# Four graph layers on one core: the SAGE products in fp16 pairs scaled on chip, and GAT's edge counts moved into its logits

## What is computed

```python
# layer 1: two SAGE layers (deg_inv = 1 / max(number of edges into a node, 1))
def _sage_layer(h, edge_src, edge_dst, deg_inv, W_self, W_neigh, b):
    agg = segment_sum(h[edge_src], edge_dst)
    return h @ W_self + (agg * deg_inv[:, None]) @ W_neigh + b
h = relu(_sage_layer(x, ..., W_self0, W_neigh0, b0))
out = _sage_layer(h, ..., W_self1, W_neigh1, b1)
# layer 2: GAT, 4 heads of 64, after rms norm and W_down
act = leaky_relu(xl[src] + xr[dst], 0.2)
e = einsum('ehd,hd->eh', act, att)
p = exp(e - segment_max(e, dst)[dst])
alpha = p / (segment_sum(p, dst)[dst] + 1e-16)
out = segment_sum(alpha * xl[src], dst) @ W_up
```

## Time and profile before

| | us |
|---|---|
| median of 3 runs | 3811.01 (3806.96 to 3817.25) |
| the profiled execution | 3811.61 |
| its span, first to last instruction | 3809.9 |
| PE busy in the span | 3487.1 |
| DVE, POOL, ACT busy | 1925.3, 1237.3, 904.2 |
| mean granted clock of PE | 0.956 |

### The profile page before, as it was taken

One profiled execution on the slowest core, in us unless ns is written; L12 is line 12 of the kernel. 1 busy time (PEld: TensorE's weight loads), 2 busy tenths in 40 slices (PEclk: granted clock), 3 DMA queues, 4 the chain that ended last, 5 costly groups with the idle time before them and its releaser, 6 DMA issues.

```text
span 3809.9 us, 55179 instructions
## 1 busy us (share of the span) xinstructions
PE 3487.1 (92%) x22747; PEld 2907.5 (76%) x22747; DVE 1925.3 (51%) x4210; ACT 904.2 (24%) x1340; POOL 1237.3 (32%) x947
## 2 busy tenths in 40 slices
PE   5899079999999799999999699999999999999988
PEld 4665058999999799987778596777777777777788
DVE  7864155221333354455545497676764444444467
ACT  0111024111201211221111394332312222222224
POOL 2677633322333027776677562200000000000021
PEclk8999589999999899999999899999999999999999
DMA  8588862556422435455544557442341222221233
GB/s 291 140 263 244 244 201 65 131 126 142 121 59 51 167 102 161 153 169 185 164 145 144 185 218 269 173 139 81 123 141 56 90 76 81 77 87 67 68 100 104
DMA packets 270889, 533.95 MB, mean 140 GB/s; under 512 B 86587, under 2 KB 135730, under 8 KB 268618
## 3 DMA queue, kind: packets, MB, share of 16 engines
q1 hardware_dynamic: 145526, 400.68, 31.0%
q0 software_dynamic: 74080, 52.74, 8.7%
q10 hardware_dynamic: 51030, 77.00, 5.8%
HBM read 352.66 MB, written 177.63 MB: 139 GB/s over the span
## 4 chain that ended last, share of the span: by engine, by line
PE 60%; DMA 12%; POOL 10%; DVE 7%; issue 6%; ACT 4%; SPq 0%; POOLq 0%; ACTq 0%; DVEq 0%
PE ps L393 40%; PE ps L721 14%; DMA EM<-ee,adr 6%; POOL gr L2151 3%; POOL EM L2141 3%; POOL gl L2151 3%; PE ps L483 3%; DMA T<-cnt,adr 2%; ACT pb L1908 2%; DVE eqj L882 1%; POOL T L2114 1%; DVE eqj L879 1%; DMA slab<-T 1%; PE ps L398 1%; ACT pt L1922 1%
## 5 line engine op out<-in xcount | busy, mean ns | idle before, releaser
L721 PE MATMUL ps<-mh,whl 128*128 128x384 f16 (+5 forms) x2560 | 528.5, 300 | 20.3 <-DVE gs L1391 14.4
L393 PE MATMUL ps<-wb,xth 128*128 128x256 f32 (+1 forms) x2560 | 460.8, 282 | 7.1 <-DVE xtl L1056 5.2
L2114 POOL DMA_INDIRECT TR<-cnt,adr x167 | 270.8, 1621 | 541.2 <-DMA TR<-cnt,adr 509.6
L393 PEld LDWEIGHTS ps<-wb,xth 128*128 128x128 f32 (+1 forms) x2560 | 389.2, 186 | 8.1 <-DVE xtl L1056 5.4
L2189 POOL TENSOR_TENSOR graw<-graw,rsb 128x1280 f32<-128x1280 f32 (+1 forms) x2 | 5.6, 2822 | 1166.8 <-DMA graw<-GD 1166.8
L721 PE MATMUL ps<-ml,whl 128*128 128x384 f16 (+5 forms) x1280 | 383.0, 299 | 0.0
L721 PEld LDWEIGHTS ps<-mh,whl 128*128 128x128 f16 (+1 forms) x2560 | 289.1, 117 | 92.7 <-issue 14.5
L393 PE MATMUL ps<-wb,xtl 128*128 128x256 f32 (+1 forms) x1280 | 358.5, 280 | 0.0
L393 PE MATMUL ps<-a,yy 128*128 128x384 f16 (+4 forms) x2560 | 343.7, 297 | 6.5 <-DVE yy L1403 5.2
L393 PE MATMUL ps<-a,xhb 128*128 128x384 f16 (+5 forms) x1280 | 341.0, 296 | 0.0
L393 PE MATMUL ps<-a,xob 128*128 128x384 f16 (+5 forms) x1280 | 339.8, 296 | 0.0
(11 more groups left out here) (308 smaller groups left out, 6974.1 us busy)
## 6 DMA issues: line engine op xcount, KB each, us to landing
TR<-zero_w SPq DMA_DIRECT2D x80, 625.0 KB, 3.8
wraw<-in_L_gnn_weight SPq DMA_DIRECT2D x64, 512.0 KB, 3.3
EM<-neg SPq DMA_DIRECT2D x10, 2500.0 KB, 21.8
ar<-TR SPq DMA_DIRECT2D x72, 320.0 KB
eb<-EM SPq DMA_DIRECT2D x9, 2500.0 KB, 9.1
ar<-TR SPq DMA_DIRECT2D x72, 305.0 KB
UD<-ue ACTq DMA_DIRECT2D x72, 256.0 KB, 3.2
uu<-UD SPq DMA_DIRECT2D x36, 512.0 KB, 6.9
```

What stands on the lines that cost most here:

```text
L393: i = pe.matmul(ap, l, r, start=(q == 0), stop=(q == len(pairs) - 1))
L721: ins = pe.matmul(ps[:, 0:cn], l, r, start=(q == 0), stop=(q == len(pairs) - 1))
L2114: return pool.indirect_dma_start(out=flat, out_offset=bass.IndirectOffsetOnAxis(ap=adr[:, n, t:t + 1], axis=0), in_=cnt[:, n, t:t + 1], in ...
```

## The change

Its parts:

1. The operands of all SAGE matmuls (am, hhi, hlo, wb, and x as xh16, xl16) are fp16. As fp16 has a small range, x1 is scaled by XS = 1024, the weights by YS = 56 over their largest magnitude, and the hidden layer by a bound made of the largest weights and the largest bias. The largest magnitudes are found on chip: SP loads every weight of a layer once more in 16 pieces of 512 KB (ww_), DVE reduces each (layer 0's in the loop over the tiles of x1, layer 1's in layer 0's finish steps), PE turns and spreads the result, and `scales` makes the scale vectors. The results are unscaled in the finish steps (und, dn).
2. Copies and subtractions of these operands turn into multiplications by a scale (ACT) and scalar_tensor_tensor (DVE).
3. In SP's order, weights of the next quarter are loaded earlier (W_neigh at the start of a quarter, W_self after its fifth tile).
4. The counts of GAT: instead of multiplying exp(e - max) by the count, log(count) is added to the logit. POOL gathers the count of each edge from BD (`times`, 167 indirect transfers between the adds to TR, from add 20 on one each, and two each in the last 20); SP reads BD's diagonal (`load_loops`, ten transfers of single elements, ahead of the first SAGE weights); DVE waits for the counts after tile 5 of x2T, ACT takes the logarithms after tile 7; DVE adds them to each batch of logits. The root for the rms norm moves from the end of x2T to its beginning.
5. In the softmax stage nb and the multiplications are gone, eb has three buffers, and the maxima of tiles 1 to 9 are taken over all heads at once by halving (m1, m2, m3), one or two tiles ahead. DVE copies the second group of pt too for heads 0 to 2. For head 3 POOL copies the logits into pb first and exp works in place. The rows of x2 for the next stage are loaded in another order.

```diff
-        am = at("am", [128, NT, N], F32R, O + 78.5)
+        am = at("am", [128, NT, N], F16, O + 78.5)
-        hhi = at("hhi", [128, NT, 256], F32R, O + 127.5)
+        hhi = at("hhi", [128, NT, 256], F16, O + 127.5)
...
+            def largest_piece(layer, j):
+                w.wait_ge(*ww_in[layer][j % 2](j))
+                dve.tensor_reduce(out=wm[:, layer, j:j + 1], in_=ww_[layer][j % 2][:, :, :], axis=AX.XY, op=ALU.max,
+                                  apply_absolute_value=True).then_inc(*V.tick("wm", layer, j))
...
-                    dve.tensor_tensor(wb[n][:, 1, :, c], wp[a][:, :, :], wb[n][:, 0, :, c].bitcast(F32),
-                                      ALU.subtract).then_inc(*V.tick("wp", w_turn[0] - 1))
+                    dve.scalar_tensor_tensor(out=wb[n][:, 1, :, c], in0=wp[a][:, :, :], scalar=ssc[:, layer, n:n + 1],
+                                             in1=wb[n][:, 0, :, c], op0=ALU.mult, op1=ALU.subtract).then_inc(
+                        *V.tick("wp", w_turn[0] - 1))
...
             for i in range(NT):
                 turned_rows("x2T", i)
+                if i == 5:
+                    rsqrt(dve, w, rms[:, :], vpe[:, :], t10[:, :], "rms")
+                    w.wait_ge(*cg_in("cg"))
+                    dve.tensor_scalar(out=cg[:, :], in0=cg[:, :], scalar1=1.0, scalar2=None, op0=ALU.max).then_inc(*V.tick("cg"))
...
+                w.wait_ge(*A("cg"))
+                dve.tensor_tensor(ee[:, t0:t0 + m, :], ee[:, t0:t0 + m, :], cg[:, t0:t0 + m, None].broadcast_to([EP, m, 4]),
+                                  ALU.add).then_inc(*V.tick("ee", b))
...
+                if part == 0:
+                    w.wait_ge(*em_in[a](i))
+                    dve.tensor_tensor(m1[0:r, :, :], eb[a][0:r, 0:625, :], eb[a][0:r, 625:1250, :], ALU.max).then_inc(*V.tick())
+                elif part == 1:
+                    dve.tensor_tensor(m2[0:r, :, :], m1[0:r, 0:313, :], m1[0:r, 312:625, :], ALU.max).then_inc(*V.tick())
+                else:
+                    dve.tensor_tensor(m3[0:r, :, :], m2[0:r, 0:157, :], m2[0:r, 156:313, :], ALU.max).then_inc(*V.tick())
...
+                if i == 7:
+
+                    w.wait_ge(*dg_in("dg"))
+                    for r, c in ((128, slice(0, 9)), (98, slice(9, 10))):
+                        act.activation(dg[0:r, c], dg[0:r, c], ACT.Ln).then_inc(*A.tick("dg"))
+                    w.wait_ge(*V("cg"))
+                    act.activation(cg[:, :], cg[:, :], ACT.Ln).then_inc(*A.tick("cg"))
...
+            def times(t):
+
+                w.wait_ge(*bd_out("bd"))
+                pool.indirect_dma_start(
+                    out=cg[:, t:t + 1], out_offset=None, in_=BD.rearrange("a b -> (a b)").rearrange("(c d) -> c d", d=1),
+                    in_offset=bass.IndirectOffsetOnAxis(ap=adr[:, 0, t:t + 1], axis=0)).then_inc(*cg_in.tick("cg"))
+
             for t in range(ET):
                 w.wait_ge(*tr_add.now())
                 w.wait_ge(*V("adr", 1, min(t // 34 * 34 + 33, ET - 1)))
                 add_counts(TR, 1, t, RPAD * N - 1).then_inc(*tr_add.tick("last"))
+                for c in range(*((t - 20, t - 19) if t < 147 else (2 * t - 167, 2 * t - 165))):
+                    if c >= 0:
+                        times(c)
...
-                    pool.tensor_tensor(pb[n][0:r, :], pb[n][0:r, :], nb[a][0:r, :], ALU.mult).then_inc(*G.tick("weighed", i, h))
...
+            def load_loops():
+                w.wait_ge(*V("rsqrt", "dis"))
+                for i in range(NT):
+                    a0, r = 128 * i * (N + 1), ROWS[i]
+                    sp.dma_start(dg[0:r, i:i + 1], BD.rearrange("a b -> (a b)").rearrange("(c d) -> c d", d=1)[
+                        a0:a0 + (r - 1) * (N + 1) + 1:N + 1, :], allow_slow_non_contiguous=True).then_inc(*dg_in.tick("dg"))
```

More of the change, by code:

```diff
@@ L48 @@
 NS, NU = 11, 4
+HS = 1024 * YS
 NMX = 16 * (NREL - NBR)
@@ L209, in program @@
         up_in, up_out = landed("up_in"), landed("up_out")
+        ww_in = [[landed(f"ww_in{layer}{i}") for i in range(2)] for layer in range(2)]
         wd_in, xl_out, ed_out = landed("wd_in"), landed("xl_out"), landed("ed_out")
@@ L491, in tensor, with largest_weights, spread_weights @@
             turn_rows("xT", 9, zt[9 % NX])
+            def largest_weights(layer):
+                ps = psum.take("wl", layer)
+                w.wait_ge(*V("wl", layer))
+                w.wait_ge(*psum.empty("wl", layer))
+                pe.transpose(ps[0:2, 0:128], wl_[:, layer, 0:2], ident[:, :]).then_inc(*P.tick("wl", layer))
+            def spread_weights(layer):
+                ps = psum.take("ws", layer)
+                w.wait_ge(*V("wlm", layer))
+                w.wait_ge(*psum.empty("ws", layer))
+                pe.matmul(ps[:, 0:2], wl_[0:2, layer, 2:3].broadcast_to([2, 128]), ident[0:2, 0:2], start=True, stop=True).then_inc(
+                    *P.tick("ws", layer))
             for d in TURN_D:
                 r = ROWS[d]
+                if d == TURN_D[1]:
+                    largest_weights(0)
+                if d == TURN_D[3]:
+                    spread_weights(0)
                 for g in range(3):
@@ L1125, in vector @@
                     V.at["hlo", layer, q] = V.n
+                    if layer == 0 and q == 2:
+                        largest_over_rows(1)
+                    if layer == 0 and q == 3:
+                        scales(1)
                     for i in range(NT):
@@ L1300, in vector @@
                 dve.tensor_copy(pt[n][0:98, 1:2, 0:r], four(ps, r)[0:98, 1:2]).then_inc(*t)
-                if h == 1:
-                    weigh_late(i)
-                if i + 1 < NT:
-                    maxima(i + 1, h)
+                for j, part in EARLY_MX.get(g, ()):
+                    maxima(j, part)
+                if i > 1 and h > 0:
+                    maxima(i + 2, h - 1)
                 if h == 2 and i > 0:
@@ L1757, in scalar @@
                         w.wait_ge(*P("hn", layer, q, i))
-                        copy(hhi[0:r, i, :], psum.at("hn", layer, q, i)[0:r, 0:256], "hhi", layer, q, i)
+                        act.mul(hhi[0:r, i, :], psum.at("hn", layer, q, i)[0:r, 0:256], 1.0 / (HS if layer else XS)).then_inc(
+                            *A.tick("hhi", layer, q, i))
                         if q == 0 and i == 8:
@@ L1914, in scalar @@
                 r = ROWS[i]
-                for k0 in range(2):
+                for k0 in range(1 if h < 3 else 2):
                     n = (3 * g + k0) % NPT
```

274 lines of the change are left out of this document (197 added, 77 removed).

## The result

The changed kernel takes 3788.0 us (median of 5 runs, 3787.39 to 3801.05), the kernel before beside it 3807.83: a ratio of 0.9956, 95% interval [0.9938, 0.9974]. So the change brings 5 to 20 us by the medians, at most about three fifths of the 32.7 forecast; 3788 lies inside the range of 3753 to 3823. The profiled execution took 3787.45 us, span 3785.7.

What follows compares the result with a forecast made beforehand. PE's matmul issue interval was taken to bound the SAGE layers, PE and GpSimd's chain nearly equally the logits. Terms -50.7 + 3 + 18 + 2 - 5 = -32.7 took 3811.6 to 3779 us, range 3753 to 3823.

Steps and rivals of the forecast that it cites:

- Step 1: SAGE matmuls in fp16: 5440 matmuls at 109.0 in place of 118.4 ns, -50.7 us, bounds 0 and -51.
- step 2: Producers of the fp16 operands on ScalarE and VectorE: covered by idle time, so nothing except at layer 0's start.
- Step 3: Search for the largest weights in both SAGE layers: extra loads and VectorE reduces cost PE nothing.
- Step 4: Start of SAGE layer 0: small VectorE instructions and ten diagonal gathers delay it, +3 us, bounds 0 and +8.
- Step 5: GpSimd's TR chain delayed by loads and gathers: counts complete at 1313 us, 15 late in x2T; +18 us, bounds 0 and +67.
- Step 6: Logarithms of the counts on ScalarE in x2T, a table load and three short instructions: +2 us, bounds 0 and +4.
- Step 7: Softmax: PE bound at 3.43 us per head, so only its start gains, -5 us, bounds 0 and -20.
- (c): Rival: softmax bound by ScalarE, -20 us in place of -5, 3764 us; chance 0.05.
- (a): Rival: loads cost the TR chain under 1 us each, counts land by 1298 in time, 3761 us; chance 0.22.
- (b): Rival: gathers queue behind adds to TR, counts land at 1360, 62 us late, 3826 us; chance 0.13.
- (d): Rival: fp16 matmul interval unchanged in the SAGE layers, nothing late, 3812 us; chance 0.05.

Runs made afterwards that it cites:

- e5: The changed kernel itself, run again in a second set beside the kernel before: 3804.91 us, ratio 0.9991.
- e6: The kernel before, unchanged, traced on the same chip as the second set of runs: median 3809.65 us.
- e10: The changed kernel without the 167 gathers of counts, counts taken as 1, weight loads kept: ratio to before 0.9933.
- e9: The kernel before with the softmax's weighing by counts (waits, loads, multiplications) left out: 3886.07 us, ratio 0.9993.
- e7: The changed kernel with VectorE's wait for the counts moved to just ahead of the logits, ScalarE's logarithm later too: 3774.61 us, ratio 0.9901.
- e8: The changed kernel with the counts' wait moved, softmax maxima reordered and GpSimd's fourth-head copies waiting for their tile's maxima: 3764.98 us, ratio 0.9873.
- e1: The changed kernel with the wait for the counts moved to just ahead of the logits, on a slower chip: 3883.4 us, ratio 0.9968.
- e4: The changed kernel without the 32 weight loads and their reduces, largest weight taken as 0.2: 3881.06 us, ratio 0.9959.
- e12: The changed kernel with the counts' wait moved and GpSimd's fourth-head copies waiting for their tile's maxima, order of maxima kept: ratio 0.9916.

## Why the forecast was right in sign and its gain too large

**Step 1 held** in its size per matmul: 109.2 ns against the forecast's 109.0. From the first SAGE matmul to the last sum it is 619.7 us in place of 666.1: -46.4 in the first pair of profiles, and -46.3 in e5 against e6 (619.4 and 665.7). Of the 4 us missing from 50.7, two are idle time of PE before these matmuls, for VectorE's low halves of x and of the weights: 9.2 us in the page's group, against 7.1 before. So "nothing" in **step 2** was 2 us too little; the other two have no row of their own. **Step 3** held: between 531 and 616 us VectorE is busy 50.8 us and PE 81.2 (82.1 before, over the same times). **Step 4** was +3 and is +0.4: from the end of the z matmuls to the first SAGE matmul 25.2 against 24.8 us. The ten loads of the diagonal took SP 4.6 us, as reckoned, and no one waited for them:

```profile
615.63 4.61 SPq L2487 DMA_DIRECT2D dg<-BD  x10
620.28 2.26 SPq L2500 DMA_DIRECT2D wp<-in_L_gnn_W_neigh  x2
```

The rule of the Trainium skill (DMA: Bandwidth & Descriptors, Rules for kernel authors), one descriptor per element, would by the forecast's estimate have put the term near +8. How long these loads took to land no row shows; they have until x2T, and the weight loads behind them on SP were not late.

**Step 5 is the step that failed, in its size.** Its mechanism is what happened. The term that was too small is the delay of the chain. It was taken as 59 us; from first to last add the chain took 882.9 us in place of 810.2 in the first pair of profiles, 73 more, and 893.5 in place of 826.9 in e5 and e6, 67 more. cg was forecast complete at 1313 us in the old trace's time and was at 1318.7 in an execution that was 6 us early: 12 us late. That is as much as the two adds lost that ran into the loads behind the SAGE layers (11.5 us), for which the forecast has no term beyond its 3 us for busy cycles; the loads' part, 45, is 52 in e10 against e9, which also runs into those loads. The forecast also rests on one trace, and that trace has the shortest chain of all that have neither loads nor gathers, by 17 us.

The other side, when the counts are needed, was about right. The forecast took it from the place where PE begins xd's second chunk, 1298. PE had gone on until 1295.2, which is 1301 in the old trace's time. So PE stood for 25.0 us where 15 were forecast, and the price was 27.5 where 18 stood; in e5, 37.5 and 38.9.

VectorE's own wait is longer than PE's, 31 us in place of the 15 that the forecast named as its sign, because VectorE runs ahead of PE. In the old trace it went on from tile 5 to the next tiles at once:

```profile
1334.30 3.67 DVE L1003 TENSOR_TENSOR xtl<-ps,xth 128x512 fp32r<-128x512 f32 x6
```

so the place of the wait was passed at 1337, not 1346, and with the 47 us of steps 1 and 4 taken off that is 1290; it asked at 1287.8. When VectorE began to wait PE still had work for 7.4 us, which count in the wait and not in its price. Between the two executions the wait and its price moved with the chain's end, which came 11 us later in e5. By the traces, one of each, that is most of why the same change was worth 20 us in one set of runs and 5 in the next.

**Step 6** held: with the wait away (e7, e8), the stage is 93.5 us against 91.1 and 91.6, some +2 us; a table load of 1.28 us and the short logarithms lie in it. **Step 7** was -5 and is -0.6: in the first pair of profiles PE's first turn came 5.4 us earlier after the eb load, exactly as forecast, and was given back by z3 (146.8 us from that turn, 142.0 before), to what the forecast's own lower bound named, the late maxima of tile 1, and those of tile 2 besides. Most of these 5 us show as slower work: over the stretch PE is idle 5.7 us in place of 5.3, but busy 141.1 in place of 136.8, at a granted clock of 0.74 over the first 40 us. My figure of 3.43 us per head was also too long: it added two busy times that overlap. In the changed kernel the weight loads start 3.28 us apart from head to head:

```profile
2217.31 1.12 PEld L422 LDWEIGHTS ps<-ident,pb 128*128 128x128 f32 x10
2218.41 2.31 PEld L417 LDWEIGHTS ps<-xlx,pt 128*128 128x128 f32 x20
2220.59 1.12 PEld L422 LDWEIGHTS ps<-ident,pb 128*128 128x128 f32 x10
```

so 40 heads are at most 131 us. In the kernel before the heads are as far apart (turns at 2187.23, 2190.51 and 2193.79 us), and the other 11 of its 142 us are 5.3 us of idle time, spread over start, tiles and end, the turns of gn (the normalised sums, once per tile), and the lower clock of the first 11 us (0.56). "Heads below 3.3 us would prove (c)" was therefore no test: they were that already. PE is the bound in the middle; the start was not, and e8 takes 7 us out of it.

**The sum** in terms measured from the first pair: -46.4 + 0.4 + 27.5 + 2.4 - 1.4 (the logits' stage, 759.5 us against 760.9 from first gather to last put) - 0.6 (last put to z3) = -18.1, against -19.8 by the medians. For e5 against e6: -46.3 - 0.1 + 38.9 + 1.9 + 7.7 (763.6 us against 755.9) - 1.9 (162.2 against 164.1) = +0.2, where the medians say -4.7. What makes the logits' stage 8 to 12 us longer than e6's in e5, e7 and e8 and 1 us shorter in the first profile stays open; one small VectorE instruction per batch was added to it, and the stage of the kernel before itself took 760.9 and 755.9 us.

**Rivals.** (a), cg in time, did not hold, but e7, whose edit makes it hold, took 3774.6 us, 35 us below before, where (a) reckoned with 51: steps 1 and 7 gave less, and the stage of logits was 11 us longer. (b), gathers behind adds, did not: gathers alone cost the chain 14 us. The rule of the Trainium skill beside it (DMA: Bandwidth & Descriptors, SWDGE vs HWDGE vs iDMA), rings served in turn, is in keeping with the loads' effect on the adds, 1.6 us for 512 KB, which is far from what (b) needed; no run shows the turns themselves. (c) fell by the changed kernel and e8, as said under e9, and (d) by the interval of 109 ns.

## What to carry to other kernels

When an edit adds a wait, read two times from the old trace. The length of the wait counts from when the waiting engine gets there, which its own timeline shows; an in-order engine that runs ahead will stand for the whole difference. The price counts from when the next engine would have needed what stands behind the wait: here 31 us of wait, 25 us of idle PE, 27.5 us of stage. Put a late value's wait as close to its first use as the program allows: here one moved wait was worth 30 us, more than half of what the fp16 operands brought. And a serial chain that ran hidden beside a stage becomes the bound when the stage gets shorter and the chain longer by the same edit; take both off the slack before the sum is made, and ask what the chain will run into once it ends later. How much a hidden chain varies does not show in the time: here it is 17 us between executions of the same code, so read it in more than one trace.

## What the runs showed of the hardware

- VectorE's maximum of two fp32 tensors (128x2500 elements) takes 2.76 us alone (e8), 4.44 us (e7) and 4.78 us (the changed kernel) when it starts during a GpSimd copy of 128x1250, and one of 128x628 takes 0.81 us alone and 2.50 beside such a copy. In both rows of e7 the copy runs on for 1.8 us, and VectorE's instruction takes 1.7 us longer: it loses nearly all of the time in which the two overlap.
- On the two chips with 3903 us, PE, ScalarE and VectorE have waits in the stage of logits that nothing in the profile ends, under "issue". The waits of e1 in its stretch of logits:

```profile
ACT ue L2017 <- issue: 48.1, 19, 19.9
PEld ps L417 <- issue: 39.8, 60, 1.1
PEld ps L654 <- issue: 28.2, 17, 6.9
```

  (us in total, times, longest). e7 has no such wait of PE in that stage. e9, which is the kernel before up to the softmax, has them too (27.5 us in 39 for its main matmuls), and needs 805 us from first gather to the last put against 756 in e6. So it is not the change. Another chain ends last there: the first eb load starts 2.2 us behind the last put in e5 to e8, but 24 to 62 us behind it in all eight traces on these chips, after PE's products for RGCN (in e1 the chain of waits runs there through L654 to L656 and ScalarE's copies of them). From first gather to first eb load it is 848 us in e9 and 758 in e6, which is nearly all of the 94 us between the chips. So a gain ahead of the stage can be lost in it where these products end last, and the small ratios of e1 to e4 and e10 to e12 say little of what the same edit is worth on the other chip. What holds the issue up, no run here shows.
